# Attention pass of a four-layer graph network: all scatters in bf16 parts, half of the turned one-hots made by ScalarE

## The chip, the cores and the metric

The kernel runs on one core of one Trainium2 chip. The metric is the device time of one execution in microseconds (us), the median of several runs.

## The reference

A graph of 6,250 nodes and 206,250 edges (sorted by destination) passes through four layers, each on the normalized and rectified node features h (64 wide), each added to x. The change concerns the first layer, graph attention with four heads:

```python
h = (x @ W).reshape(n, HEADS, CH)
a_src = jnp.einsum('nhc,hc->nh', h, att_src)
a_dst = jnp.einsum('nhc,hc->nh', h, att_dst)
e = leaky_relu(a_src[src] + a_dst[dst], NEG_SLOPE)
e = jnp.exp(e - m[dst])                      # m: an upper value per node
alpha = e / (segment_sum(e, dst) + 1e-16)
out = segment_sum(h[src] * alpha[:, :, None], dst)
```

The three layers behind it (a mean over neighbours, a weighted sum, and two relational convolutions) are not touched.

## The kernel before, in words

**Windows and groups.** The destinations are cut into 49 windows of 128 nodes (WINDOWS). A first pass sorts the edges so that each window has 50 slots-columns of 128 edges (CPW): one column for each block of 128 source nodes and one more. The columns of a window are handled in six groups (NG) of 10, 8, 8, 8, 8, 8 columns (GS, starting at G0). "Group g of window dx" is written (dx, g) here; it is number dx*6+g. Groups 0 to 2 add into one PSUM bank, groups 3 to 5 into another.

**One group.** Gathering and scattering are matrix products with one-hot matrices.

- SyncE loads the group's codes (two rows, source and destination place, broadcast to 128 partitions) into BC, one of three buffers, number g % 3 (line 533).
- `turned_one_hots` (line 2183) compares them with the partition's own number and so makes the turned one-hots OT, 2 x GS[g] x 128 bf16 values in a partition, in one VectorE instruction (line 2190). It waits for the codes (f_bc), for SyncE's copy of what the same OT buffer held before (f_kept), and for the gather that read it (f_gath).
- SyncE writes the first half of OT to DRAM for the third layer (`keep`, line 523). In SyncE's loop (line 530) the load for (dx, g) waits until the turned one-hots three groups before are made, and right behind it stands the keep of those one-hots.
- TensorE gathers (line 1325 and 1327): per column three products with the parts of h and three with the parts of the destination's table.
- VectorE takes the larger of two scores (`scores`, line 2205), ScalarE the exponential (line 930), VectorE weighs the rows with it (`weigh`, line 2213).
- VectorE makes the untransposed one-hots ODb (`one_hots`, whose instruction stands in the helper `compare`, line 1844).
- TensorE scatters. In groups 0, 1, 3, 4 (g % 3 < 2) the weighed f32 rows are split into three bf16 parts: the first is the upper half of the word, VectorE makes the second (`rest`, line 2222), GpSimd the third (`lowest_part`, line 751), and TensorE runs three bf16 products a column (line 1343). In groups 2 and 5 the rows stay f32 (Wf), ScalarE turns the one-hots into f32 (`one_hots_whole`, line 937) and TensorE runs one f32 product a column (line 1349).
- Three odd edges per partition are added at the window's end (`few` makes their one-hots, line 2235; the products, line 1356), and VectorE adds the two banks to the sums (`evict`, line 2232).

**Order.** Every engine's order is written out by hand; nothing is planned by a program. For each g, TensorE runs the gather of the group three further on and then the scatter of g. VectorE runs (line 2239, `body`): weigh(g); turned one-hots of the group four further on; rest(g) if g % 3 < 2; scores(g+1); one_hots(g+1); and an evict after g = 2 and g = 5, few after g = 3. ScalarE runs, for each g: the slot codes for `one_hots` (line 944) at g = 2 and 5, the exponential of g+1, and `one_hots_whole` of g+1. GpSimd runs the four lowest parts and a small copy of the window's table (line 745). "Step g" below is VectorE's work from weigh(g) up to weigh(g+1).

Of the kernel before, what the change touches and what calls it, by code (L numbers as in the profile page):

```python
# [15 lines left out]
P = 128  # L16
# [4 lines left out]
LASTW = WINDOWS - 1  # L21
# [101 lines left out]
def gnn_stack(nc, x, src, dst, etype, eweight, w0, att_src, att_dst, bias0, gamma0, beta0, w1t, b1, w2t, b2,  # L123
# [11 lines left out]
    with ctx:  # L135
# [179 lines left out]
        OD = cv.take(GS[2] * P).rearrange("p (k n) -> p k n", n=P)  # L315
        WV = DIM + HEADS
        Wf = cv.take(GS[2] * WV).rearrange("p (k c) -> p k c", c=WV)
        W3 = [cv.take(GS[a] * PARTS * WV).rearrange("p (k a c) -> p k a c", a=PARTS, c=WV) for a in range(2)]
# [105 lines left out]
        f_oht, f_ohb, f_ohd, f_gath, f_whole = (sem(n) for n in ("f_oht", "f_ohb", "f_ohd", "f_gath", "f_whole"))  # L424
        f_tab, p_rest, p_low = sem("f_tab"), sem("p_rest"), sem("p_low")
# [44 lines left out]
        def weighed(g):  # L470

            return Wf if g % 3 == 2 else W3[g % 3][:, 0:GS[g], 0, :]

        def in_parts(dx, g):

            return dx * 4 + (g // 3 * 2 + g % 3 + 1)
# [4 lines left out]
        def _(sp):  # L481
# [43 lines left out]
            def load_codes():  # L525
# [18 lines left out]
                for g in range(3, NG):  # L544
                    sp.wait_ge(f_oht, LASTW * NG + g + 4)
                    keep(LASTW, g)
# [48 lines left out]
        def _(pool):  # L595
# [143 lines left out]
            with pool.Else():  # L739
# [19 lines left out]
                lowest_part(0, 1)  # L759
                pool.wait_ge(f_mg, 16 * 2 * MC)  # L760
# [4 lines left out]
                lowest_part(0, 4)  # L765
                pool.wait_ge(f_mexp, 1)
# [5 lines left out]
                with pool.Fori(1, LASTW) as d:  # L772
# [3 lines left out]
                    lowest_part(d, 3)  # L776
                    lowest_part(d, 4)
                for g in (0, 1, 3, 4):
                    lowest_part(LASTW, g)
# [39 lines left out]
        def _(act):  # L819
# [296 lines left out]
        def _(pe):  # L1116
# [190 lines left out]
            def gather(dx, g):  # L1307
# [4 lines left out]
                pe.wait_ge(f_oht, n + 4)  # L1312
# [18 lines left out]
            def scatter(dx, g):  # L1331
# [4 lines left out]
                if g % 3 < 2:  # L1336
                    pe.wait_ge(p_low, in_parts(dx, g))
                    pe.wait_ge(f_ohb, n + 1)
# [1228 lines left out]
```

## Time and profile before

| | us |
|---|---|
| median of 3 runs (4734.94 to 4755.01) | 4735.81 |
| the profiled execution, its own time | 4763.33 |
| its span, first to last instruction | 4761.2 |
| the attention pass in it | about 1030 to 1911 |

The profiled execution is 27.5 us above the median and 2.1 us above its own span. A row of the profile names the line of the kernel, the engine, the operation, what it writes and reads, how often it ran, its busy time, the mean of one in ns, and how long the engine had been idle before it and what released it. PE is TensorE's products, PEld its loads of weights, DVE VectorE, ACT ScalarE, POOL GpSimd, SP SyncE. The recorded duration of an instruction reaches beyond the start of the next one on the same engine by some 0.08 us (VectorE) to 0.09 us (ScalarE), so what an instruction costs its engine is the step from its start to the next start.

### The profile page before, as it was taken

To read this page: it belongs to the slowest core of one execution; us is meant where nothing else is said; L and a number is where in the kernel's file an instruction comes from. 1 tells how busy PE (TensorE), PEld (TensorE's weight loads), DVE (VectorE), ACT (ScalarE), POOL (GpSimd) and SP (SyncE) were. 2 spreads that over 40 slices of the span, in tenths; PEclk is the share of its full clock that TensorE was granted. 3 is DMA by queue.
4 is the path that set the end of the run, shared out by engine and by line. 5 is a ranking of instruction groups with operands and counts; after the bars stand their busy time and mean duration, and the time that the engine had idled before them with its cause. 6 is when DMAs were issued, how large, how long until landed. Compare 5 with 4: busy or idle time off the path is not lost.

```text
span 4761.2 us, 259988 instructions
## 1 busy us (share of the span) xinstructions
PE 4240.2 (89%) x103202; PEld 3795.6 (80%) x103202; DVE 4055.6 (85%) x6401; ACT 3062.0 (64%) x10437; POOL 827.5 (17%) x952
## 2 busy tenths in 40 slices
PE   1899999839999999499969999699999989999998
PEld 1677777639999999488869999588888868888887
DVE  7799999989999999899989999877767766767666
ACT  2899999802222222487779999666666656666665
POOL 2355555413333334000000000000000000000000
PEclk7999999969999999799989999899999989999999
DMA  1000000048888887000025555333333333333333
GB/s 55 2 2 2 2 2 2 2 117 280 276 281 277 280 277 255 15 0 0 0 67 144 147 143 146 89 98 96 98 97 98 97 87 101 99 100 99 101 96 83
DMA packets 305220, 501.36 MB, mean 105 GB/s; under 512 B 76918, under 2 KB 78454, under 8 KB 305126
## 3 DMA queue, kind: packets, MB, share of 16 engines
q1 hardware_dynamic: 303782, 499.39, 35.4%
q8 instruction: 64, 1.05, 0.1%
q0 software_dynamic: 576, 0.52, 0.1%
q10 hardware_dynamic: 768, 0.16, 0.0%
q14 instruction: 30, 0.25, 0.0%
HBM read 408.40 MB, written 91.57 MB: 105 GB/s over the span
## 4 chain that ended last, share of the span: by engine, by line
PE 44%; DVE 24%; issue 13%; ACT 13%; POOL 3%; DVEq 1%; DMA 1%; ACTq 0%; POOLq 0%; SPq 0%
PE PS L1535 20%; ACT arena L869 11%; PE PS L1528 9%; DVE arena L1844 7%; DVE arena L2454 4%; POOL arena L751 3%; PE PS L1327 3%; PE PS L1325 3%; PE PS L1343 2%; DVE arena L2288 2%; DVE arena L2293 2%; PE PS L1349 2%; PE PS L1566 1%; PE PS L1449 1%; PE PS L1464 1%
## 5 line engine op out<-in xcount | busy, mean ns | idle before, releaser
L1844 DVE TENSOR_TENSOR arena<-iotab,arena 128x1024 bf16<-128x1024 bf16 (+4 forms) x1887 | 1605.2, 882 | 188.5 <-PE PS L1535 166.7
L1076 ACT ACTIVATE arena<-PS 128x384 bf16<-128x384 f32 x2450 | 1004.1, 501 | 544.5 <-PE PS L1528 540.9
L1535 PE MATMUL PS<-arena 32*128 32x193 bf16 (+1 forms) x41552 | 998.2, 242 | 47.0 <-DVEq L2455 42.1
L1535 PEld LDWEIGHTS PS<-arena 32*128 32x128 bf16 x41552 | 840.5, 93 | 151.6 <-DVEq L2455 59.1
L869 ACT ACTIVATE arena<-PS,m 128x196 bf16<-128x196 f32 x1813 | 740.6, 445 | 22.0 <-PE PS L1184 21.9
L1528 PE MATMUL PS<-Hp,arena 128*128 128x192 bf16 (+1 forms) x4900 | 537.9, 249 | 35.3 <-DVE Hp L1688 35.0
L1045 ACT ACTIVATE arena<-PS,ewB 128x64 f32<-128x64 f32 x2450 | 526.4, 479 | 34.7 <-PE PS L1388 34.7
L1325 PE MATMUL PS<-Hp,arena 128*128 128x72 bf16 x7350 | 499.2, 198 | 42.1 <-DVE arena L2190 40.9
L1327 PE MATMUL PS<-arena 128*128 128x72 bf16 x7350 | 499.8, 198 | 0.0
L1528 PEld LDWEIGHTS PS<-Hp,arena 128*128 128x128 bf16 x4900 | 383.2, 99 | 146.0 <-issue 84.4
L930 ACT ACTIVATE arena<-arena 128x32 f32<-128x32 f32 (+1 forms) x294 | 68.3, 232 | 648.2 <-DVE arena L2205 645.3
L1191 PE MATMUL PS<-arena,tmp 128*128 128x262 bf16 x1813 | 452.0, 278 | 15.9 <-DVE tmp L1844 13.7
L1184 PE MATMUL PS<-agg,identb 128*128 128x196 bf16 x1813 | 449.9, 248 | 0.0
L1325 PEld LDWEIGHTS PS<-Hp,arena 128*128 128x128 bf16 x7350 | 411.9, 101 | 42.3 <-DVE arena L2190 41.0
L869 ACT ACTIVATION_READ_ACCUMULATOR arena<-PS,m 128x1 f32 x1813 | 412.4, 227 | 0.0
L1327 PEld LDWEIGHTS PS<-arena 128*128 128x128 bf16 x7350 | 405.0, 100 | 0.0
L751 POOL TENSOR_TENSOR arena<-arena 128x680 f32<-128x680 f32 x196 | 325.9, 1663 | 369.8 <-DVE arena L2222 369.0
L1009 ACT ACTIVATE arena<-PS 128x1024 bf16<-128x1024 f32 (+1 forms) x294 | 311.1, 1059 | 94.0 <-PE PS L1449 87.1
L1388 PE MATMUL PS<-Hp,arena 128*128 128x64 bf16 x7350 | 265.0, 194 | 25.0 <-DVE Hp L1688 20.0
L719 POOL DMA_INDIRECT arena<-rows_h,midx x12 | 15.3, 1275 | 1564.3 <-DMA rows_h<-Hn 1516.2
L2454 DVE TENSOR_REDUCE arena<-PS 128x512 f32<-128x1536 f32 x98 | 171.8, 1753 | 129.9 <-PE PS L1535 129.9
L1183 PE MATMUL PS<-Hp,own_b 128*128 128x196 bf16 x1045 | 262.0, 251 | 22.8 <-ACT arena L869 21.2
(374 smaller groups left out, 8298.0 us busy)
## 6 DMA issues: line engine op xcount, KB each, us to landing
arena<-hots SPq DMA_DIRECT2D x735, 256.0 KB, 2.6
arena<-codes SPq DMA_DIRECT2D x245, 512.0 KB, 5.2
hots<-arena SPq DMA_DIRECT2D x245, 256.0 KB, 5.1
arena<-hots SPq DMA_DIRECT2D x147, 320.0 KB
arena<-codes SPq DMA_DIRECT2D x49, 640.0 KB, 5.4
hots<-arena SPq DMA_DIRECT2D x49, 320.0 KB, 5.4
rows_h<-Hn SPq DMA_DIRECT2D x4, 1568.0 KB, 9.2
rows_l<-Y SPq DMA_DIRECT2D x1, 1764.0 KB, 9.8
```

The lines of the kernel that those rows point to most:

```text
L751: pool.tensor_tensor(W3[a][:, 0:n, 2, :], W3[a][:, 0:n, 1, :], W3up[a][:, 0:n, 1, :], ALU.subtract).then_inc(p_low, 1)
L869: act.activation(junk[:, j % 4, :], ps[j % 4][:, 0:KEYS], ACT.Relu, bias=m256[:, 0:1], accum_out=rank[par][:, j:j + 1]).then_inc(k_rank, 1)
L1045: done = act.activation(W3q[g][:, k, 0, :], bank_at(g, k), ACT.Copy, scale=ewB[:, bass.ds(dx * CPW + (G0[g] + k), 1)])
L1076: act.activation(RG[ROW_BUFFER[g]][:, 2 * i:2 * i + 2, 0:RW], ps[PAIR_BANK[q]][:, 0:2 * RW].rearrange("p (k c) -> p k c", k=2), ACT.Copy). ...
L1184: pe.matmul(to, identb[:, j:j + 1].to_broadcast((P, P)), Tb[par], start=False, stop=True).then_inc(k_pref, 1)
L1191: pe.matmul(ps[4][:, 0:EW + 2], OS[:, j, :], E[:, j, 0:EW + 2], start=(j == 0), stop=(j == NJ - 1)).then_inc(k_perm, 1)
L1325: pe.matmul(to, OT[g % 3][:, k * P:(k + 1) * P], rhs, start=(a == 0), stop=False)
L1327: last = pe.matmul(to, OT[g % 3][:, (sz + k) * P:(sz + k + 1) * P], ztab[:, a, :], start=False, stop=(a == PARTS - 1))
L1528: last = pe.matmul(ps[PAIR_BANK[q]][:, (c % 2) * RW:(c % 2 + 1) * RW], rOT[hot][:, (c - G0[hot]) * P:(c - G0[hot] + 1) * P], rhs, start=Tr ...
L1535: last = pe.matmul(ps[2 + q][:, b * SW:b * SW + SW - o], one_hot[32 * q:32 * q + 32, b * P:(b + 1) * P], rows_of[32 * q:32 * q + 32, 0:SW ...
L1844: return dve.tensor_tensor(to.rearrange("p k (n t) -> p k n t", t=4), iota_of[:, 0:n].rearrange("p (n t) -> p n t", t=4)[:, None, :, :] .t ...
L2454: flink(dve.tensor_reduce(Zs.rearrange("p (q b) c -> p q b c", b=2), sums, AX.X, ALU.add))
```

## The change

Groups 2 and 5 are scattered in bf16 parts like the others: the f32 one-hots OD, the rows Wf, `one_hots_whole` and the f32 products go; a third buffer W3[2] comes, and `rest` and `lowest_part` now run for all six groups. The turned one-hots of groups 0, 2 and 4 stay with VectorE. Those of groups 1, 3 and 5 are made by ScalarE: `codes_away` writes the distance |p + 1 - code| over the codes in BC, and `turned_one_hots` writes relu(1 - distance) to OT. Two semaphores (f_away, f_ota) are added; `wait_turned` picks f_oht or f_ota for TensorE and SyncE.

```diff
         def in_parts(dx, g):
-            return dx * 4 + (g // 3 * 2 + g % 3 + 1)
+            return dx * NG + (g + 1)
+
+        def wait_turned(engine, dx, g):
+            engine.wait_ge(f_ota if g % 2 else f_oht, dx * 3 + (g // 2 + 1))
...
# SyncE, load of the codes
                     for g in range(NG):
-                        sp.wait_ge(f_oht, dx * NG + g + 1)
+                        if g >= 3:
+                            wait_turned(sp, dx, g - 3)
+                        elif not first:
+                            wait_turned(sp, dx - 1, g + 3)
...
# GpSimd
-                    lowest_part(d, 3)
-                    lowest_part(d, 4)
+                    for g in range(2, NG):
+                        lowest_part(d, g)
...
# ScalarE
-            def one_hots_whole(dx, g):
-
-                if g % 3 == 2:
-                    act.wait_ge(f_ohb, dx * NG + g + 1)
-                    act.wait_ge(f_scat, dx * NG + g + 1)
-                    act.activation(OD, ODb[2], ACT.Copy).then_inc(f_ohd, 1)
+            def codes_away(dx, g):
+
+                act.wait_ge(f_bc[g % 3], dx * 32 + (g // 3 + 1) * 16)
+                of = BC[g % 3][:, 0:2 * GS[g] * P]
+                act.activation(of, of, ACT.Abs, bias=pidx[:, 1:2], scale=-1.0).then_inc(f_away, 1)
+
+            def turned_one_hots(dx, g):
+
+                act.wait_ge(f_away, dx * 3 + (g // 2 + 1))
+                if g >= 3 or not is_zero(dx):
+                    act.wait_ge(f_kept[g % 3], dx * 32 + g // 3 * 16)
+                act.wait_ge(f_gath, dx * NG + g + 1)
+                m = 2 * GS[g] * P
+                act.activation(OT[g % 3][:, 0:m], BC[g % 3][:, 0:m], ACT.Relu, bias=ones[:, 0:1],
+                               scale=-1.0).then_inc(f_ota, 1)
...
                     slot_codes(cdw, 0, h, None)
+                codes_away(0, 1)
+                turned_one_hots(0, 1)
+                codes_away(0, 3)
+                turned_one_hots(0, 3)
                 exponents(0, 0)
-                one_hots_whole(0, 0)
...
                         if g < NG - 1:
                             exponents(dx, g + 1)
-                            one_hots_whole(dx, g + 1)
                         elif not last:
                             exponents(dx + 1, 0)
-                            one_hots_whole(dx + 1, 0)
+                        if g == 0:
+                            codes_away(dx, 5)
+                        elif g == 1:
+                            turned_one_hots(dx, 5)
+                        elif g % 2 == 0 and not last:
+                            codes_away(dx + 1, g - 1)
+                        elif not last:
+                            turned_one_hots(dx + 1, g - 2)
...
# TensorE, scatter: all groups as g % 3 < 2 before
-                else:
-                    pe.wait_ge(f_whole, n + 3)
-                    pe.wait_ge(f_ohd, dx * 2 + (h + 1))
-                    for k in range(GS[g]):
-                        last = pe.matmul(to, OD[:, k, :], Wf[:, k, :], start=False,
-                                         stop=(g == 2 and k == GS[g] - 1))
...
# VectorE
                         weigh(dx, g)
-                        if g < NG - 4:
-                            turned_one_hots(dx, g + 4)
-                        elif not last:
-                            turned_one_hots(dx + 1, g + 4 - NG)
-                        if g % 3 < 2:
-                            rest(dx, g)
+                        if g == 0:
+                            turned_one_hots(dx, 4)
+                        elif g % 2 == 0 and not last:
+                            turned_one_hots(dx + 1, g - 2)
+                        rest(dx, g)
...
-                for g in range(4):
+                for g in (0, 2):
                     turned_one_hots(0, g)
```

## Rows read from the trace of the kernel before

**Rows 1.** Page, busy us and share of the span by engine

```profile
PE 4240.2 (89%) x103202; PEld 3795.6 (80%) x103202; DVE 4055.6 (85%) x6401; ACT 3062.0 (64%) x10437; POOL 827.5 (17%) x952
```

**Rows 2.** Stretch 1247 to 1423: busy us (instructions) by engine, clock, DMA share, GB/s

```profile
1247.00:1423.00 176.00, 174.04 (x4393) 172.79 (x4390) 176.00 (x311) 38.66 (x100) 70.02 (x50) 1.00 0.87 279
```

**Rows 3.** Line 2235 (`few`, once a window) from 1070 to 1882

```profile
L2235 DVE TENSOR_TENSOR arena<-iota,mrel x46: 1445/1448/1452, 1072.7 to 1866.7; 128x384 f32<-128x384 f32 x46
```

**Rows 4.** Groups by line and form, 1036 to 1911: busy us, mean ns | idle before, releaser

```profile
L751 POOL TENSOR_TENSOR arena<-arena 128x544 f32<-128x544 f32 x147 | 236.1, 1606 | 181.4 <-DVE arena L2222 180.6
L2190 DVE TENSOR_SCALAR arena<-arena,pidx 128x2048 bf16<-128x2048 bf16 x245 | 215.9, 881 | 5.2 <-DMA hots<-arena 3.1 <-DMA arena<-codes 2.1
L1343 PE MATMUL PS<-arena 128*128 128x68 bf16 x4998 | 191.6, 194 | 13.4 <-POOL arena L751 13.3
L751 POOL TENSOR_TENSOR arena<-arena 128x680 f32<-128x680 f32 x49 | 89.8, 1833 | 188.4 <-DVE arena L2222 188.4
L2190 DVE TENSOR_SCALAR arena<-arena,pidx 128x2560 bf16<-128x2560 bf16 x48 | 53.4, 1113 | 0.0
```

**Rows 5.** Chain that ended last, 1490 to 1526: start, us, what

```profile
1492.67 0.76 PE PS L1343 x24
...
1503.76 1.81 PE PS L1349 x16
```

**Rows 6.** VectorE in order of time, parts of steps 2, 3, 5 and 0: start, us

```profile
1491.66 1.11 DVE L2190 TENSOR_SCALAR arena<-arena,pidx 128x2560 bf16<-128x2560 bf16 x1
...
1494.16 0.74 DVE L2190 TENSOR_SCALAR arena<-arena,pidx 128x2048 bf16<-128x2048 bf16 x1
1494.82 0.71 DVE L2222 TENSOR_TENSOR arena<-arena 128x544 f32<-128x544 f32 x1
1495.45 0.21 DVE L2205 TENSOR_REDUCE arena<-PS 128x32 f32<-128x64 f32 x1
1495.59 0.68 DVE L1844 TENSOR_TENSOR arena<-iotab,arena 128x1024 bf16<-128x1024 bf16 x1
1496.19 1.45 DVE L2235 TENSOR_TENSOR arena<-iota,mrel 128x384 f32<-128x384 f32 x1
1497.56 0.68 DVE L2213 TENSOR_TENSOR arena<-PS,arena 128x512 f32<-128x512 f32 x1
...
1501.84 0.81 DVE L1844 TENSOR_TENSOR arena<-iotab,arena 128x1280 bf16<-128x1280 bf16 x1
1502.57 0.21 DVE L2232 TENSOR_TENSOR agg<-agg,PS 128x68 f32 x1
1502.70 0.81 DVE L2213 TENSOR_TENSOR arena<-PS,arena 128x640 f32<-128x640 f32 x1
1503.43 0.74 DVE L2190 TENSOR_SCALAR arena<-arena,pidx 128x2048 bf16<-128x2048 bf16 x1
1504.10 0.85 DVE L2222 TENSOR_TENSOR arena<-arena 128x680 f32<-128x680 f32 x1
1504.87 0.21 DVE L2205 TENSOR_REDUCE arena<-PS 128x32 f32<-128x64 f32 x1
```

**Rows 7.** ScalarE in order of time, the exponential of group 1

```profile
1505.12 0.23 ACT L930 ACTIVATE arena<-arena 128x32 f32<-128x32 f32 x1 [2.93 <-DVE arena L2205]
```

**Rows 8.** SyncE, one load of codes and the keep behind it

```profile
1492.93 0.38 SPq L533 DMA_DIRECT2D arena<-codes  x1
1493.50 0.36 SPq L523 DMA_DIRECT2D hots<-arena  x1
```

**Rows 9.** Line 523 (keep), the whole trace

```profile
DMA to landing us min/median/max: 2.0/5.1/6.7
```

**Rows 10.** Lines of ScalarE, by form: busy us, mean ns

```profile
L937 ACT ACTIVATE arena<-arena 128x1024 f32<-128x1024 bf16 x98 | 103.8, 1059 | 36.0 <-DVE arena L1844 36.0
L930 ACT ACTIVATE arena<-arena 128x32 f32<-128x32 f32 x245 | 56.7, 231 | 614.8 <-DVE arena L2205 611.9 <-PE PS L1343 2.9
L834 ACT ACTIVATE st<-st,epsc 128x28 f32<-128x28 f32 x5 | 1.6, 321 | 1.8 <-DVE st L1652 1.8
L949 ACT ACT_TABLE_LOAD x1 | 1.3, 1283 | 35.2 <-DVEq L2014 35.2
```

**Rows 11.** The pass begins: VectorE in order of time, waiting for first transfers

```profile
1034.83 0.89 DVE L2190 TENSOR_SCALAR arena<-arena,pidx 128x2560 bf16<-128x2560 bf16 x1 [5.49 <-DMA arena<-codes]
1042.45 0.75 DVE L2190 TENSOR_SCALAR arena<-arena,pidx 128x2048 bf16<-128x2048 bf16 x1 [3.11 <-DMA hots<-arena]
```

**Rows 12.** Line 533 (load of codes), its first three, 1020 to 1034

```profile
DMA to landing us min/median/max: 4.7/4.7/4.7
```

More of the change, by code:

```diff
@@ L314, in gnn_stack @@
         ODb = [cv.take(GS[a] * P, bf16).rearrange("p (k n) -> p k n", n=P) for a in range(3)]
-        OD = cv.take(GS[2] * P).rearrange("p (k n) -> p k n", n=P)
         WV = DIM + HEADS
-        Wf = cv.take(GS[2] * WV).rearrange("p (k c) -> p k c", c=WV)
-        W3 = [cv.take(GS[a] * PARTS * WV).rearrange("p (k a c) -> p k a c", a=PARTS, c=WV) for a in range(2)]
+        W3 = [cv.take(GS[a] * PARTS * WV).rearrange("p (k a c) -> p k a c", a=PARTS, c=WV) for a in range(3)]
         W3up = [v.rearrange("p k a c -> p (k a c)").bitcast(bf16).rearrange(
@@ L424, in gnn_stack @@
         f_oht, f_ohb, f_ohd, f_gath, f_whole = (sem(n) for n in ("f_oht", "f_ohb", "f_ohd", "f_gath", "f_whole"))
+        f_away, f_ota = sem("f_away"), sem("f_ota")
         f_tab, p_rest, p_low = sem("f_tab"), sem("p_rest"), sem("p_low")
@@ L544, in load_codes @@
                 for g in range(3, NG):
-                    sp.wait_ge(f_oht, LASTW * NG + g + 4)
+                    wait_turned(sp, LASTW, g)
                     keep(LASTW, g)
@@ L759, in _ @@
                 lowest_part(0, 1)
+                lowest_part(0, 2)
                 pool.wait_ge(f_mg, 16 * 2 * MC)
@@ L765, in _ @@
                 lowest_part(0, 4)
+                lowest_part(0, 5)
                 pool.wait_ge(f_mexp, 1)
@@ L775, in _ @@
                     table_of(d + 1)
-                    lowest_part(d, 3)
-                    lowest_part(d, 4)
-                for g in (0, 1, 3, 4):
+                    for g in range(2, NG):
+                        lowest_part(d, g)
+                for g in range(NG):
                     lowest_part(LASTW, g)
@@ L1311, in gather @@
                 m = sz // 2
-                pe.wait_ge(f_oht, n + 4)
+                wait_turned(pe, dx, g)
                 if g == 0:
@@ L1335, in scatter @@
                 to = ps[4 + h][:, 0:WV]
-                if g % 3 < 2:
-                    pe.wait_ge(p_low, in_parts(dx, g))
-                    pe.wait_ge(f_ohb, n + 1)
-                    if g % 3 == 0:
-                        pe.wait_ge(f_accout, dx * 2 + (h + 1))
-                    for k in range(GS[g]):
-                        for a in range(PARTS):
-                            last = pe.matmul(to, ODb[g % 3][:, k, :], W3up[g % 3][:, k, a, :],
-                                             start=(g % 3 == 0 and k == 0 and a == 0), stop=False)
-                else:
-                    pe.wait_ge(f_whole, n + 3)
-                    pe.wait_ge(f_ohd, dx * 2 + (h + 1))
-                    for k in range(GS[g]):
-                        last = pe.matmul(to, OD[:, k, :], Wf[:, k, :], start=False,
-                                         stop=(g == 2 and k == GS[g] - 1))
+                pe.wait_ge(p_low, in_parts(dx, g))
+                pe.wait_ge(f_ohb, n + 1)
+                if g % 3 == 0:
+                    pe.wait_ge(f_accout, dx * 2 + (h + 1))
+                for k in range(GS[g]):
+                    for a in range(PARTS):
+                        last = pe.matmul(to, ODb[g % 3][:, k, :], W3up[g % 3][:, k, a, :],
+                                         start=(g % 3 == 0 and k == 0 and a == 0),
+                                         stop=(g == 2 and k == GS[g] - 1 and a == PARTS - 1))
                 last.then_inc(f_scat, 1)
@@ L2196, in one_hots @@
                         dve.wait_ge(f_codes, dx * 2 + (g // 3 + 1))
-                    if g % 3 < 2:
-                        dve.wait_ge(f_scat, dx * NG + (g + 1))
-                    elif not (is_zero(dx) and g < 3):
-                        dve.wait_ge(f_ohd, dx * 2 + g // 3)
+                    dve.wait_ge(f_scat, dx * NG + (g + 1))
                     compare(ODb[g % 3][:, 0:GS[g], :], iotab1, cdw[:, G0[g]:G0[g] + GS[g], :]).then_inc(f_ohb, 1)
@@ L2274, in attention_pass @@
                 dve.wait_ge(f_accout, 2 * WINDOWS + 2)
-                dve.sem_inc(f_ohd, 4 * WINDOWS)
+                dve.sem_inc(f_ohd, 6 * WINDOWS)
             def weight_pass():
@@ L2342, in _ @@
             with dve.Else():
-                dve.sem_inc(f_oht, 3)
                 dve.sem_inc(f_whole, 2)
```

3 lines of the change are left out of this document (1 added, 2 removed).

## Prediction, written before the changed kernel was run

> **What bounds the kernel now.** I read the page's first part, then one steady stretch of the attention pass, then the groups of the pass by line, then the order of time on each engine, and the two DMA lines last. Over the whole kernel no engine is full [rows 1]; inside the pass two are: in 176 us VectorE is busy 176.00 and TensorE 174.04, TensorE's granted clock is 1.00 (2.4 GHz), the DMA engines are busy 0.87 of the time and ScalarE only 38.66 us [rows 2]. `few` runs once a window and its starts lie (1866.7 - 1072.7) / 45 = 17.64 us apart [rows 3]: that is the price of a window. VectorE never waits in it, TensorE waits 13.3 us in 49 windows, 0.27 each, for GpSimd [rows 4]. So both engines need some 17.4 to 17.6 us a window, and a change that relieves only one gains nothing. This one relieves both, and loads ScalarE, GpSimd and the turnaround of the buffers.
>
> **TensorE.** An f32 scatter of eight columns occupies it for 1.81 us, a bf16 one in three parts for 0.76 [rows 5]. Two of them change: -2.10. It then needs 17.64 - 0.27 - 2.10 = 15.27 us a window.
>
> **VectorE, without new waits.** Turned one-hots now: five of 2048 elements at 0.881 and one of 2560 at 1.113 [rows 4]; less the overlap of 0.08 that the steps show (0.74 recorded, 0.66 to the next start [rows 6]) that is 5.04 us. The mean is above 0.74 because an instruction that starts while GpSimd's L751 runs is drawn out (the 1.11 of rows 6). After: two of 2048 at 0.66 and one of 2560 at 0.89 - 0.08 = 0.81 [rows 6, 11], 2.13 us; I count no drawing out, since GpSimd's 1.61 us after `rest` are over, or nearly, before the next of them starts. That is -2.91. Two more `rest` at 0.63 [rows 6]: +1.26. In steps 1, 3 and 5 `rest` now stands right behind weigh and waits for its completion: weigh is recorded with 0.68, the next could start after 0.60, and with 0.03 for the signal that is 0.11 each, +0.33. Sum: 17.64 - 2.91 + 1.26 + 0.33 = **16.32 us**.
>
> **ScalarE.** The two f32 one-hots (1059 ns) go. Six instructions of 2048 elements come. Between 32 and 1024 elements an ACTIVATE rises by (1059 - 231) / 992 = 0.835 ns an element, so 2048 take 1059 + 1024 x 0.835 = 1914 ns; the new ones take their bias from a column, and L834, which does, takes 321 ns for 28 elements against 231 for 32: +0.09, so 2.00 us [rows 10]. Bounds: 1.91 without that term, 2.1 with twice the term. Less the overlap of 0.09 that is 6 x 1.91 = 11.5 us, with exponentials and slot codes some 12.7 us a window: not the bound. The Trainium skill, ScalarE: Activation LUTs, "Rules for kernel authors", speaks against such a move: it gives relu-like work to VectorE, up to three times as fast in bf16. The rows agree for one instruction (2.00 against 0.74) and two are needed here; it costs nothing as long as ScalarE's time is spare, but it costs latency, which is the next point.
>
> **The turnaround of the OT buffers.** This is the term that decides. VectorE writes OT for the group four further on, and it must wait until what the buffer held has been written to DRAM (f_kept). Before, the buffer's former content was made three steps earlier by VectorE itself, which left room for the landing of the keep. Now VectorE's one-hots of (dx+2, 0), in step 2 of window dx+1, go into the buffer that ScalarE filled with (dx+1, 3), and ScalarE starts that only behind the exponential of (dx+1, 0), that is after scores at the end of step 5. From the end of those scores:
>
> - exponential: 0.04 until it starts [rows 6, 7], 0.23 - 0.09 until the next can start; the one-hots 2.00 [rows 10];
> - SyncE: the turned one-hots of 1491.66 ended at 1492.77 and the load was issued at 1492.93, so 0.16 [rows 6, 8]; the keep stands 0.57 behind the load [rows 8];
> - landing of the keep 5.1, the median [rows 9]; 0.03 for the signal.
>
> Sum 0.04 + 0.14 + 2.00 + 0.16 + 0.57 + 5.1 + 0.03 = **8.04 us**. VectorE's work from the same moment to those one-hots [rows 6]: one_hots(0) 0.65 left, evict 0.13, weigh(0) 0.73, turned (4) 0.67, rest(0) 0.77, scores 0.14, one_hots(1) 0.60, weigh(1) 0.60, rest(1) 0.11 + 0.63, scores 0.14, one_hots(2) 0.60, weigh(2) 0.60: **6.37 us**. So VectorE waits 8.04 - 6.37 = 1.67 us. The same sum for buffer 1 (filled behind scores(4), wanted in step 0) is 7.61 of work, `few` with 1.37 lying in it, and a wait of 0.43; that wait lies inside the 8.04 of the first and shortens its wait to 1.24, so the total stays 1.67. Buffer 2 has 7.48 and the 1.24: no wait.
>
> A window is then 16.32 + 1.67 = **17.99 us**, against 17.64: +0.35, in the 48 windows that make one-hots for a next one +16.8 us. TensorE (15.27) and the DMA engines (0.87 x 17.64 / 17.99 = 0.85) are below it. GpSimd has 5 x 1.61 + 1.83 [rows 4] and the table's copy, some 10.3 us; groups 2 and 5 now wait for it too, which costs TensorE time that it has.
>
> **The start.** Today VectorE's fourth turned one-hots start at 1042.45, released by a keep [rows 11]. Now they are ScalarE's, and the first exponential stands behind them: their 2.00 against 0.66 puts it back by 1.3 us, and by some 1.9 more if the distance is not finished by then. I take 1.9, between these. The end of the pass I cost at nothing.
>
> **Sum.** +16.8 + 1.9 = +18.7 us. The profiled execution took 4763.3, its successor would take 4782.0; the median of the runs shown stands 27.5 lower, so 4735.8 + 18.7 = **4754.5 us**. The unknown is the landing of the keep: a tenth of a us is worth 4.8 us. Its recorded ends are 2.0 and 6.7 [rows 9]; I take the median, since the load ahead of this keep is the large one but the queue has had some 5 us to empty. The pass's first load, the same 640 KB on an empty queue, needed 4.7 [rows 12]; the keep behind it is issued 0.57 later and adds 256 KB, at 279 GB/s [rows 2] 0.9 us: 4.7 - 0.57 + 0.9 = 5.0.
>
> **Rivals.** About 0.5% (24 us) is what a measurement of this kernel can tell from no change.
>
> 1. *The keep lands in time (faster), 15%.* If it lands in 3.4 us or less the wait is gone, and VectorE's 16.32 set the window: 48 x -1.32 + 1.9 = -61, 4674 us. For it: in the fast case nothing is queued. Against it: medians of 5.1 now, and 4.7 for a transfer on an empty queue. Over 4.2 us the gain is within 0.5%. The Trainium skill, DMA: Bandwidth & Descriptors, "Anatomy of one DMA", gives about 2.0 us plus bytes at 436 GB/s; by it load and keep together would need 4.1 us, the keep 3.5 from its own issue, and the window would be 16.4 us, 4679 us in all, an estimate from that page. The trace disagrees where it can be compared: that page makes 3.5 us of the first load, the row 4.7.
> 2. *The keeps land later (slower), 36%.* ScalarE ends odd one-hots after VectorE has ended the next even ones, so SyncE sends two loads and two keeps in a row, 1664 KB within 1.6 us. If they share the DMA engines instead of following each other, the keep lands a us later, 6.1, still under the 6.7 seen; the window is 18.99 and the time 4735.8 + 64.8 + 1.9 = 4802 us. It decides from 5.2 us on, where +0.5% is reached, very near my forecast; hence its large share.
> 3. *Table loads, 2%.* If Abs or Relu needed another table than Exp, each change of table would cost 1.28 us [rows 10], two a group: ScalarE would need 12.7 + 12 x 1.28 = 28.1 us a window, +500 us, 5238 us. Against it: Copy and Exp alternate in this pass, and the one load is ahead of it [rows 10]. The Trainium skill, ScalarE: Activation LUTs, "Table sets: the hidden batching unit", has relu and abs in every set.
>
> **How the numbers follow.** My forecast, a keep landing between 4.2 and 5.2 us, has 47%, and its own range is 4712 to 4760. Rival 1 has 15%, rival 2 36%, rival 3 2%. Faster by over 0.5%: 0.15; within: 0.47; slower: 0.38. The range reaches into rival 1 to 4702 (a landing of 4.0) and to 4802 for rival 2; the bounds of ScalarE's instruction (-0.09 to +0.1, 5 us) lie inside.
>
> **What would show it.** VectorE's L2190 with idle time ahead of it, released by the DMA that writes `hots`, about 1.2 us in step 2 and 0.4 in step 0; `few` 18.0 us apart; ScalarE's new lines at 2.0 us; SyncE's transfers in pairs; TensorE idle over 2 us a window; no ACT_TABLE_LOAD in the pass. VectorE without idle time and 16.3 us between the `few`s would make the forecast wrong, as would waits for scores or exponentials.

## The result, and the profile after

The changed kernel takes **4836.47 us** (median of 4 runs, 4831.0 to 4838.03) against 4735.72 for the kernel before beside it: a ratio of 1.0202 [1.0183, 1.0221]. It is slower by 2.0%, and outside the range of the prediction (4702 to 4802). The profiled execution took 4838.03 us, with a span of 4836.3.

The page's first part and the stretch of the pass answer to [rows 1, 2]; the window is read from `few`, now line 2252, as in [rows 3]. Columns as there.

```profile
PE 4159.9 (86%) x103986; PEld 3705.7 (77%) x103986; DVE 4035.7 (83%) x6352; ACT 3520.0 (73%) x10633; POOL 962.6 (20%) x1050
...
1250.00:1426.00 176.00, 147.18 (x4204) 143.54 (x4205) 158.33 (x276) 123.55 (x130) 89.73 (x65) 0.99 0.83 258
...
L2252 DVE TENSOR_TENSOR arena<-iota,mrel x46: 1442/1443/1446, 1075.3 to 1944.3; 128x384 f32<-128x384 f32 x46
```

No engine is full any more: in 176 us TensorE went from 174.04 to 147.18 and VectorE from 176.00 to 158.33. The window is (1944.3 - 1075.3) / 45 = **19.31 us** where 17.99 was forecast. At the granted clock of 0.99 the TensorE clock has no part in this. The first `few` starts at 1055.3, where it was 1055.0, and the last at 1981.3, where it was 1900.6: 80.7 us later, 80.4 of them in the 48 windows. After it the kernel is shorter by 5.6. So the whole loss arose in the pass. The windows are not alike: from one `few` to the next it is 18.6 to 20.2 us, but for the last, so what one stretch of the trace shows lies about the mean.

The groups of the pass by line and form, 1036 to 2000 (as [rows 4]; 2239 is `rest`, 2210 VectorE's turned one-hots, 944 and 953 ScalarE's two steps, 1368 the scatter in three parts):

```profile
L2239 DVE TENSOR_TENSOR arena<-arena 128x544 f32<-128x544 f32 x245 | 218.4, 891 | 5.1
...
L953 ACT ACTIVATE arena<-arena,ones 128x2048 bf16<-128x2048 bf16 x147 | 294.3, 2002 | 0.4
L944 ACT ACTIVATE arena<-arena,pidx 128x2048 bf16<-128x2048 bf16 x147 | 292.1, 1987 | 6.7 <-DMA arena<-codes 6.7
...
L2210 DVE TENSOR_SCALAR arena<-arena,pidx 128x2560 bf16<-128x2560 bf16 x48 | 42.5, 886 | 67.1 <-DMA hots<-arena 63.2 <-PE PS L1353 3.1 <-DMA arena<-codes 0.8
L2210 DVE TENSOR_SCALAR arena<-arena,pidx 128x2048 bf16<-128x2048 bf16 x98 | 72.9, 744 | 28.3 <-DMA hots<-arena 25.3 <-DMA arena<-codes 2.1 <-issue 0.4
```

Two things stand here. VectorE waits 63.2 + 25.3 = 88.5 us for transfers that write `hots`, some 1.8 us a window. And the mean `rest` of 544 elements takes 891 ns, where the one of [rows 6] took 0.71: 245 x 0.18 = 44 us, 0.9 a window, that no wait shows.

VectorE in order of time, parts of steps 4, 5 and 0 to 2 (as [rows 6]):

```profile
1497.76 0.71 DVE L2239 TENSOR_TENSOR arena<-arena 128x544 f32<-128x544 f32 x1
...
1499.84 0.90 DVE L2239 TENSOR_TENSOR arena<-arena 128x544 f32<-128x544 f32 x1
1500.66 0.23 DVE L2222 TENSOR_REDUCE arena<-PS 128x40 f32<-128x80 f32 x1
...
1503.24 0.75 DVE L2210 TENSOR_SCALAR arena<-arena,pidx 128x2048 bf16<-128x2048 bf16 x1 [0.74 <-DMA hots<-arena]
...
1505.42 0.68 DVE L2230 TENSOR_TENSOR arena<-PS,arena 128x512 f32<-128x512 f32 x1
1506.13 1.12 DVE L2239 TENSOR_TENSOR arena<-arena 128x544 f32<-128x544 f32 x1
...
1510.39 0.89 DVE L2210 TENSOR_SCALAR arena<-arena,pidx 128x2560 bf16<-128x2560 bf16 x1 [1.80 <-DMA hots<-arena]
```

GpSimd beside it, in order of time:

```profile
1492.81 1.09 POOL L757 TENSOR_TENSOR arena<-arena 128x544 f32<-128x544 f32 x1
...
1498.55 1.61 POOL L757 TENSOR_TENSOR arena<-arena 128x544 f32<-128x544 f32 x1 [2.39 <-DVE arena L2239]
...
1504.85 1.83 POOL L757 TENSOR_TENSOR arena<-arena 128x680 f32<-128x680 f32 x1 [2.27 <-DVE arena L2239]
```

The `rest` at 1497.76 has no GpSimd work beside it and takes 0.71. Those at 1499.84 and 1506.13 start while line 757 of the group before still runs, and end late: 1506.13 begins inside 1504.85 to 1506.68 and ends at 1507.25, which is 0.57 after GpSimd's end, nearly a whole `rest` (0.63 by its cadence). That is the pattern of the 1.11 of [rows 6]. GpSimd is held up in its turn: the same 544 elements take it 1.09 or 1.61. Every `rest` now has line 757 of the group before close by, and in the odd steps, where no turned one-hots of VectorE stand between, the two meet.

ScalarE and SyncE from the end of the scores at 1500.89, the path that the prediction rests on (as [rows 7, 8]), and the landing of the keep, line 526, over the trace (as [rows 9]):

```profile
1500.93 0.24 ACT L938 ACTIVATE arena<-arena 128x40 f32<-128x40 f32 x1
1501.14 2.00 ACT L953 ACTIVATE arena<-arena,ones 128x2048 bf16<-128x2048 bf16 x1
...
1503.31 0.38 SPq L539 DMA_DIRECT2D arena<-codes  x1
1503.89 0.36 SPq L526 DMA_DIRECT2D hots<-arena  x1
1504.49 0.38 SPq L539 DMA_DIRECT2D arena<-codes  x1
1505.06 0.42 SPq L526 DMA_DIRECT2D hots<-arena  x1
1509.87 0.38 SPq L539 DMA_DIRECT2D arena<-codes  x1
...
DMA to landing us min/median/max: 2.3/5.9/7.3
```

The chain is the forecast one, to the step: exponential, ScalarE's second step, load, keep, landing, and VectorE's one-hots at 1510.39 behind 1.80 us of idle time. The transfers go in pairs, with nothing for 4.8 us after them. The median keep lands 5.9 us after its issue, where it was 5.1 before; the keep of this window, issued at 1503.89, took 6.50 to the one-hots.

### The profile page after: what moved, and what is told of

The parts are those of the page before. It is cut to its first block, busy times and chain, and to the rows that moved or that the text cites. A ratio compares the mean times of both kernels' runs of the same rounds, so it can differ in the third digit from the quotient of the medians.

```text
span 4836.3 us, 261743 instructions
## 1 busy us (share of the span) xinstructions
PE 4159.9 (86%) x103986; PEld 3705.7 (77%) x103986; DVE 4035.7 (83%) x6352; ACT 3520.0 (73%) x10633; POOL 962.6 (20%) x1050
## 3 DMA queue, kind: packets, MB, share of 16 engines
q8 instruction: 64, 1.05, 0.1%
## 4 chain that ended last, share of the span: by engine, by line
PE 38%; DVE 23%; issue 17%; ACT 13%; POOL 5%; DMA 2%; DVEq 1%; ACTq 0%; POOLq 0%; SPq 0%
PE PS L1555 20%; ACT arena L877 12%; PE PS L1548 9%; DVE arena L1864 6%; POOL arena L757 5%; DVE arena L2469 4%; DVE arena L2304 2%; DVE arena L2309 2%; PE PS L1368 2%; PE PS L1353 1%; PE PS L1351 1%; DMA hots<-arena 1%; PE PS L1586 1%; PE PS L1484 1%; PE PS L1469 1%
## 5 line engine op out<-in xcount | busy, mean ns | idle before, releaser
L757 POOL TENSOR_TENSOR arena<-arena 128x544 f32<-128x544 f32 (+1 forms) x294 | 466.1, 1585 | 320.7 <-DVE arena L2239 320.7
L1368 PE MATMUL PS<-arena 128*128 128x68 bf16 x7350 | 285.6, 195 | 166.6 <-POOL arena L757 165.6
L1353 PEld LDWEIGHTS PS<-arena 128*128 128x128 bf16 x7350 | 408.7, 101 | 0.0
L1368 PEld LDWEIGHTS PS<-arena 128*128 128x128 bf16 x7350 | 252.0, 97 | 186.5 <-POOL arena L757 141.5
L944 ACT ACTIVATE arena<-arena,pidx 128x2048 bf16<-128x2048 bf16 x147 | 292.1, 1987 | 6.7 <-DMA arena<-codes 6.7
L953 ACT ACTIVATE arena<-arena,ones 128x2048 bf16<-128x2048 bf16 x147 | 294.3, 2002 | 0.4
```

The lines of the kernel that those rows point to most:

```text
L757: pool.tensor_tensor(W3[a][:, 0:n, 2, :], W3[a][:, 0:n, 1, :], W3up[a][:, 0:n, 1, :], ALU.subtract).then_inc(p_low, 1)
L1353: last = pe.matmul(to, OT[g % 3][:, (sz + k) * P:(sz + k + 1) * P], ztab[:, a, :], start=False, stop=(a == PARTS - 1))
L1368: last = pe.matmul(to, ODb[g % 3][:, k, :], W3up[g % 3][:, k, a, :], start=(g % 3 == 0 and k == 0 and a == 0), stop=(g == 2 and k == GS[g] ...
```

## The experiments

The theory: a window is VectorE's work (16.3 us, with `few` in it at 1.37), plus two terms: the turnaround of the OT and BC buffers, and the drawing out of VectorE's instructions beside GpSimd's third parts. The rivals: that the turnaround alone makes the loss; that TensorE's waits for GpSimd (165.6 us in the pass) do; that the place of `rest` does. The diffs are against the changed kernel (that of run 12 against run 8), cut to their core. Runs 1 to 4, 5 to 8 and 9 to 12 went together, with medians of the kernel before of 4747.2, 4736.9 and 4737.7; across these sets compare the ratios, since the first had the kernel before 10 us slower.

| run | median us | ratio to before | window us |
|---|---|---|---|
| changed kernel | 4836.5 | 1.0202 [1.0183, 1.0221] | 19.31 |
| 1 six OT buffers | 4815.4 | 1.0142 [1.0116, 1.0167] | 18.79 |
| 2 six OT, six BC | 4760.0 | 1.0026 [1.0013, 1.0038] | 17.61 |
| 3 `rest` late | 4821.3 | 1.0155 [1.0130, 1.0181] | 18.90 |
| 4 runs 2 and 3 together | 4775.7 | 1.0053 [1.0030, 1.0077] | 17.97 |
| 5 bf16 parts alone | 4854.8 | 1.0245 [1.0219, 1.0270] | 19.70 |
| 6 ScalarE's one-hots alone | 4842.7 | 1.0220 [1.0195, 1.0246] | 19.38 |
| 7 run 2, short third parts | 4699.0 | 0.9915 [0.9890, 0.9940] | 16.59 |
| 8 run 2, group 2 in f32 | 4716.2 | 0.9953 [0.9938, 0.9969] | 16.79 |
| 9 before, unchanged | 4742.0 (one) | - | 17.28 |
| 10 table copy later | 4836.1 | 1.0207 [1.0190, 1.0224] | 19.33 |
| 11 run 2, table copy later | 4734.9 | 0.9991 [0.9978, 1.0004] | 17.21 |
| 12 run 8, whole one-hots later | 4688.5 | 0.9896 [0.9880, 0.9913] | 16.26 |

**1. Six OT buffers, so that no one-hots wait for a keep of the same window.**

```diff
         OT = [cv.take(2 * GS[0] * P, bf16) for _ in range(3)]
+        in_tmp = tmp[:, :, :].rearrange("p w c -> p (w c)")
+        OT += [in_tmp[:, n * GS[3] * P:(n + 1) * GS[3] * P].bitcast(bf16) for n in range(3)]
...
-                if g >= 3 or not is_zero(dx):
-                    act.wait_ge(f_kept[g % 3], dx * 32 + g // 3 * 16)
-                act.wait_ge(f_gath, dx * NG + g + 1)
+                if not is_zero(dx):
+                    act.wait_ge(f_kept[g], dx * 16)
+                    act.wait_ge(f_gath, dx * NG + g - 2)
```

> The changed kernel with six OT buffers in place of three (three of them in a tensor that is idle in this pass), so that one-hots wait for a keep that is a window old. Theory (the window is set by the way from ScalarE's exponential over its one-hots and the keep to VectorE's next one-hots, 8.85 us in the trace, of which VectorE waits 2.05): the keep leaves the way and the load of codes, issued 0.57 us earlier and landing some 0.3 sooner, takes its place: 8.0 us, the wait falls to about 1.2, the window from 19.29 to 18.4, the time to about 4794 us. Rival 1 (only the keep matters): no wait left, 17.2 us, 4738. Rival 2 (the drawn-out rests and GpSimd set the pace): no change, 4836.

The waits for `hots` are gone, but the window fell by 0.52 us only. By form, VectorE's turned one-hots of group 0 now wait for the codes, 42.9 us in place of 63.2:

```profile
L2212 DVE TENSOR_SCALAR arena<-arena,pidx 128x2560 bf16<-128x2560 bf16 x48 | 43.2, 901 | 47.4 <-DMA arena<-codes 42.9 <-PE PS L1355 4.5
```

The BC buffer has the same turnaround, one transfer earlier in the queue; a wait had stood behind the wait. The time missed its expectation by some 20 us, and more drawing out goes with it: the compare of one_hots has a mean of 718 ns, against 677 where it is undisturbed (run 10).

**2. Six OT and six BC buffers; SyncE loads a window ahead.**

```diff
+        in_Y = Y[:, :, :].rearrange("p w c -> p (w c)")
+        BC += [in_Y[:, n * GS[3] * P:(n + 1) * GS[3] * P].bitcast(bf16) for n in range(3)]
...
+                        wait_turned(sp, dx, g)
+                        if not last:
+                            load(dx + 1, g)
+                        keep(dx, g)
```

> Six OT and six BC buffers; SyncE loads the codes of a group for the next window as soon as its one-hots are made. Theory: no wait is left on VectorE, the window is VectorE's own work with the rests drawn out, 16.32 + 0.91 = 17.2 us, the time 4836 - 48 x 2.05 = about 4738 us, DMA share about 0.93. Rival (the DMA engines, busy 0.83 of 19.3 us = 16.0 us a window, are the bound once transfers can queue): window 17.2 or more with VectorE waiting for codes.

But for one wait at the start of the pass VectorE no longer waits for a transfer, and the window fell by 1.70 us, to 17.61. That is the price of the turnaround: the 2.0 us of waits of the changed kernel, less what the drawing out takes back. It is 0.4 above the 17.2 expected, since more is drawn out than in the changed kernel: the mean `rest` of 544 elements takes 1002 ns, where it was 891. In order of time, VectorE and GpSimd:

```profile
1499.83 0.97 DVE L2213 TENSOR_SCALAR arena<-arena,pidx 128x2048 bf16<-128x2048 bf16 x1
1500.72 1.61 DVE L2242 TENSOR_TENSOR arena<-arena 128x544 f32<-128x544 f32 x1
...
1498.85 2.90 POOL L760 TENSOR_TENSOR arena<-arena 128x544 f32<-128x544 f32 x2
```

GpSimd had waited for the table's copy; its two third parts then run in one, 1498.85 to 1501.75, and VectorE's one-hots take 0.97 in place of 0.74 and the `rest` 1.61 in place of 0.71, ending 0.58 after GpSimd.

**3. `rest` behind scores and one_hots of the next group, in the odd steps.**

```diff
-                        rest(dx, g)
+                        if g % 2 == 0:
+                            rest(dx, g)
                         if g < NG - 1:
                             scores(dx, g + 1)
                             one_hots(dx, g + 1)
...
+                        if g % 2:
+                            rest(dx, g)
```

> The changed kernel with three buffers of each, but in the odd steps VectorE runs rest behind scores and one_hots of the next group, when GpSimd has ended the third part of the group before. Theory: the rests fall from 0.90, 1.13 and 1.02 to 0.71 us (-0.91) and the 0.11 behind weigh go (-0.33), but what of it lies on the way to the keep (0.41 + 0.11) turns into waiting: -0.7 us a window, 4836 - 35 = about 4801 us. Rival 1 (a shared port between VectorE and GpSimd does not explain the long rests, or they only moved): no change. Rival 2 (the third parts come later and hold TensorE up): slower than 4836.

By form (1864 is the compare of one_hots):

```profile
L1864 DVE TENSOR_TENSOR arena<-iotab,arena 128x1024 bf16<-128x1024 bf16 x245 | 196.6, 803 | 0.0
L2239 DVE TENSOR_TENSOR arena<-arena 128x544 f32<-128x544 f32 x245 | 177.6, 725 | 0.1
```

The `rest`s are back at 725 ns, and the compares rose instead, to 803 where an undisturbed one takes 677 (run 10). `few` came down to 0.55 in most windows, and the waits for `hots` rose to take that up. The drawing out moved to whatever stands next to GpSimd's work; the window gained 0.41 us where the theory gave it 0.7.

**4. Runs 2 and 3 together.**

> Both together: six OT and BC buffers, and rest behind one_hots in the odd steps. Theory: VectorE's work alone, 16.0 us a window, would give 4836 - 48 x 3.3 = 4678 us; the DMA engines need 16.0 us as well, so 16.0 to 16.9 and 4678 to 4722 us, faster than the kernel before. Rival (GpSimd's chain or TensorE, 15.3 us, binds): over 17 us, with TensorE's scatters waiting for L757 and VectorE waiting for the scatters.

A clear miss: the window was 17.97, slower than run 2 without the move. In its trace the drawing out stands at the turned one-hots (means of 1333 and 973 ns in place of 0.89 and 0.74) and at the `rest`s (894 ns). The theory that the place of `rest` is to blame falls with runs 3 and 4: which instruction is hit depends on the order, that some are hit does not.

**5. bf16 parts alone: all turned one-hots by VectorE, as before the change.**

```diff
         def wait_turned(engine, dx, g):
-            engine.wait_ge(f_ota if g % 2 else f_oht, dx * 3 + (g // 2 + 1))
+            engine.wait_ge(f_oht, dx * NG + (g + 1))
...
+                        if g < NG - 4:
+                            turned_one_hots(dx, g + 4)
+                        elif not last:
+                            turned_one_hots(dx + 1, g + 4 - NG)
```

> First half of the change alone: all six groups scattered in bf16 parts, all turned one-hots still made by VectorE. Theory: VectorE is the bound. Of its 17.64 us before, 1.8 are drawing-out by GpSimd (0.94 on turned one-hots, 0.89 on few); two more rests are +1.27 and two more third parts draw out more, 0.4 to 0.9: 19.3 to 19.8 us a window, +80 to +105 us against the kernel before, no waits for DMA. Rival (relieving TensorE by 2.1 us a window is worth something by itself): not slower than before.

```profile
1250.00:1426.00 176.00, 150.23 (x4095) 146.90 (x4096) 176.00 (x296) 17.59 (x72) 94.39 (x63) 0.94 0.81 250
...
1309.94 1.44 DVE L1852 TENSOR_TENSOR arena<-iotab,arena 128x1024 bf16<-128x1024 bf16 x1
```

VectorE is busy all of the 176 us and waits for no transfer: the window is 19.70. This part by itself puts 2.06 us on the 17.64 of [rows 3] (2.42 on the 17.28 of run 9). The two `rest`s are 1.27 of it; turned one-hots stand between weigh and `rest` in every step here, so there are no completion waits. Most of what is left is one compare of one_hots, in step 3, that takes 1.44 us in place of 0.68, in 42 windows. Half the change, then, only costs where VectorE is the bound; TensorE's 2.10 us went into idle time.

**6. ScalarE's one-hots alone: groups 2 and 5 scattered in f32, with their one-hots converted by ScalarE.**

```diff
+            def one_hots_whole(dx, g):
+
+                if g not in IN_PARTS:
+                    act.wait_ge(f_ohb, dx * NG + g + 1)
+                    act.wait_ge(f_scat, dx * NG + g + 1)
+                    act.activation(OD, ODb[2], ACT.Copy).then_inc(f_ohd, 1)
...
                             exponents(dx, g + 1)
+                            one_hots_whole(dx, g + 1)
```

> Second half alone: turned one-hots of groups 1, 3 and 5 by ScalarE in two steps, groups 2 and 5 scattered in f32 as before. Theory: VectorE's own work is 14.1 us, 1.3 more with GpSimd's drawing-out, and the way to the keep is the same 8.9 us, so some 2.1 us of waiting: 17.5 us a window; TensorE needs 17.4. So 17.4 to 17.9, within 0.5% of the kernel before. Rival 1 (without the way to the keep): the same, set by TensorE alone, and VectorE never waits for hots. Rival 2 (ScalarE, now 14.6 us busy, sets it): VectorE waits for L930's successor, over 18 us.

The window was 19.38 where 17.4 to 17.9 had been expected. ScalarE in order of time, and VectorE's weigh behind it:

```profile
1313.20 1.06 ACT L946 ACTIVATE arena<-arena 128x1024 f32<-128x1024 bf16 x1 [0.37 <-DVE arena L1881]
1314.16 1.99 ACT L952 ACTIVATE arena<-arena,pidx 128x2048 bf16<-128x2048 bf16 x1
1316.06 0.27 ACT L969 ACTIVATE arena<-cdA 128x96 bf16 x1
1316.23 0.22 ACT L939 ACTIVATE arena<-arena 128x40 f32<-128x40 f32 x1
...
1316.48 0.82 DVE L2247 TENSOR_TENSOR arena<-PS,arena 128x640 f32<-128x640 f32 x1 [1.55 <-ACT arena L939]
```

The scores of group 0 end at 1313.91, and their exponential starts at 1316.23, 2.3 us later, since ScalarE works in order and is in the middle of long instructions. VectorE waits 1.55 us for it, and all that follows on the path of the keep is late by as much. In the changed kernel the exponential starts 0.04 behind the scores. Of the difference, 1.34 us is ScalarE's: with the f32 one-hots in between (1.06, and 0.37 of waiting for them), it is 3.63 us from one exponential to the next (1312.60 to 1316.23), against 2.29 (1498.64 to 1500.93) in the changed kernel. The other 0.94 is VectorE's, which has no `rest` in step 5 and so ends its scores earlier. So the two halves need each other, and each alone is no better than both (1.0245, 1.0220, 1.0202).

**7. Run 2, with the third part made by GpSimd for the first column only; those of the other columns are left out.**

```diff
+                    n = 1
                     pool.tensor_tensor(W3[a][:, 0:n, 2, :], W3[a][:, 0:n, 1, :], W3up[a][:, 0:n, 1, :],
```

> Six OT and BC buffers as in e2_both6, and GpSimd computes the third part of the first column of each group only (the third parts of the other columns are left out, so TensorE adds stale values there). Theory (GpSimd's tensor_tensor draws out VectorE's instructions that read two operands from SBUF or run at the fast rate, about 2 us a window wherever they stand): rests 0.71, few 0.55, turned one-hots 0.74 all together, the window 15.4 to 16.2 us, bound by TensorE (15.3), the DMA engines (about 15.4 to 16) and VectorE (15.4) alike: 4760 - 48 x 1.4 to 2.2 = 4655 to 4693 us. Rival (the long rests come from ScalarE's accesses or from their own order): rests stay at 0.9 to 1.6, time near 4760.

```profile
L761 POOL TENSOR_TENSOR arena<-arena 128x68 f32<-128x68 f32 x294 | 181.6, 630 | 348.8 <-DVE arena L2243 348.8
...
L2243 DVE TENSOR_TENSOR arena<-arena 128x544 f32<-128x544 f32 x245 | 181.3, 740 | 5.2
```

With GpSimd's instructions down from about 1.6 to 0.63 us, the `rest`s take 740 ns, where they took 1002 in run 2, `few` 0.55 and the turned one-hots 0.75 to 0.88, and the window goes from 17.61 to 16.59. That misses the 15.4 to 16.2 expected. Most of the drawing out is gone: VectorE's instructions are shorter by some 1.8 us a window than in run 2. Waits for TensorE's scatters took part of its place (38.3 us in the pass against 9.2, 0.6 a window). So the drawing out is worth at least 1.0 us a window here. This shows GpSimd's work to be its cause: VectorE's and ScalarE's instructions are the same in both runs.

**8. Run 2, with group 2 alone in f32.** The edit is that of run 6, with IN_PARTS = (0, 1, 3, 4, 5), on run 2.

> Six OT and BC buffers, group 5 in bf16 parts, group 2 in f32 as in the kernel before (GpSimd has five third parts, VectorE five rests). Theory: VectorE 14.8 us and some 1.7 of drawing-out, TensorE 15.27 + 1.05 = 16.3 and its waits: 16.5 to 17.0 us a window, 48 x 0.6 to 1.1 below e2_both6: 4707 to 4731 us, faster than the kernel before. Rival (what holds e2 at 17.6 is the DMA engines): near 4760, VectorE or ScalarE waiting for codes.

It came out at 16.79 us a window, 0.9953 of before. What VectorE waits for now is the exponential (line 943, 44.8 us in 50 waits), which stands behind ScalarE's f32 one-hots.

**9. The kernel before, unchanged, for a second profile.**

> The kernel before, unchanged, for a second profile: its timed runs lie at 4734 to 4763 us and the first profile was taken in one of 4763. Theory (the drawing-out by GpSimd depends on where its third parts fall among VectorE's instructions, and the loop can settle in more than one pattern): if this run is again near 4760, the same 17.64 us a window; if it is near 4735, some 17.1 us a window, with few or a turned one-hot shorter. Rival (the difference lies in another stage): 17.64 us a window in a run near 4735, and another stage some 25 us shorter.

`few` is 17.28 us apart over the same 45 windows that give 17.64 in [rows 3], and takes 0.55 us, not 1.45:

```profile
L2235 DVE TENSOR_TENSOR arena<-iota,mrel x48: 541/550/1450, 1073.3 to 1884.8; 128x384 f32<-128x384 f32 x48
...
1505.34 0.55 DVE L2235 TENSOR_TENSOR arena<-iota,mrel 128x384 f32<-128x384 f32 x1
1505.81 0.68 DVE L2213 TENSOR_TENSOR arena<-PS,arena 128x512 f32<-128x512 f32 x1
1506.41 1.23 DVE L2190 TENSOR_SCALAR arena<-arena,pidx 128x2048 bf16<-128x2048 bf16 x1
```

One kernel settles into more than one pattern. In this one GpSimd meets the turned one-hots (1.23), in the one of [rows 6] it meets `few` (1.45). From the first `few` to the last it is 829.9 us against 845.6, so 15.7 less, and the whole executions differ by 21 (4763.3 and 4742.0). The timed runs of the kernel before fall apart in the same way: of the nine beside runs 5 to 8, seven lie at 4733.5 to 4737.6 and two at 4755.3 and 4756.9. At 17.28 TensorE is full (176.00 us of the 176 from 1250 to 1426), where it was busy 174.04 in [rows 2].

**10. The table's copy behind the third part of group 2, three buffers.**

```diff
                     lowest_part(d, 1)
+                    lowest_part(d, 2)
                     table_of(d + 1)
-                    for g in range(2, NG):
+                    for g in range(3, NG):
                         lowest_part(d, g)
```

> The changed kernel with three buffers of each and one step of GpSimd moved: the table's copy, which waits for a gather, stands behind the third part of group 2 in place of ahead of it, so that TensorE's scatter of group 2 need not wait for both. TensorE's waits for GpSimd (165 us in the pass) should shrink by some 40 to 80 us. Theory (the way to the keep sets the window): these waits cover nothing, the time stays at 4836 within 10 us. Rival (GpSimd's chain holds TensorE up and that sets the window): over 20 us faster.

The time is unchanged, as the theory said. But it is a weak test of the rival: TensorE's waits for line 757, which should have shrunk by 40 to 80 us, stayed as they were (165.7 us in 141 waits, against 165.6 in 142), and only GpSimd's own wait for the gather went. That TensorE's waits are slack rests on the changed kernel's own trace, where VectorE waits for the gather and the scatters some 8 us in the whole pass and 88.5 for the keeps, and on run 2, where the window fell by 1.70 us with the same third parts.

**11. Run 2 with the edit of run 10.**

> Six OT and BC buffers as in e2_both6, with the same move of the table's copy. Without the way to the keep, VectorE waited 0.14 us a window there for TensorE's scatters, and the pattern jumped between windows (17.61 on average, up to 0.35 about it). Theory: 17.2 to 17.6 us a window, 4740 to 4760 us. Rival (GpSimd's chain was the hidden bound of e2): under 17.0, under 4731 us.

```profile
L2243 DVE TENSOR_TENSOR arena<-arena 128x544 f32<-128x544 f32 x245 | 207.2, 846 | 5.1
```

Without the transfers' waits the same edit is worth 0.40 us a window, at the upper end of what was expected (17.2 to 17.6 us): GpSimd's two third parts no longer run in one, and the 1.61 of run 2 is gone. At 0.9991 [0.9978, 1.0004] it is level with the kernel before. `few` is drawn out again, to 1.44.

**12. Run 8, with ScalarE's f32 one-hots of group 2 behind the exponential of group 3.**

```diff
                             exponents(dx, g + 1)
-                            one_hots_whole(dx, g + 1)
+                            if g == 2:
+                                one_hots_whole(dx, 2)
```

> As e8_hybrid2 (six buffers, group 2 in f32, group 5 in parts), but ScalarE turns the one-hots of group 2 into f32 behind the exponential of group 3 in place of ahead of the distances' second step. In e8 VectorE waited 0.9 us a window in weigh(3) for that exponential (L943). Theory: that wait goes, TensorE with 16.3 us of work and its own waits is the bound: 16.4 to 16.6 us a window, 4716 - 48 x 0.2 to 0.4 = 4697 to 4706 us. Rival (the f32 one-hots come too late for TensorE): not faster than 4716.

```profile
1250.00:1426.00 176.00, 176.00 (x4850) 176.00 (x4847) 174.90 (x314) 152.47 (x162) 88.60 (x66) 1.00 0.95 303
```

16.26 us a window and 4688.5 us, 0.9896 [0.9880, 0.9913] of before, somewhat better than expected (16.4 to 16.6), and the time beats both kernels. TensorE is full, VectorE 174.90 of 176 and the DMA engines 0.95: this keeps most of the change, with one group left in f32, one long instruction of ScalarE out of the exponentials' way, and buffers for all six groups.

## Why the prediction was wrong

Of the mechanism one half was right: a new wait for `hots`, in steps 0 and 2, on the path named, is the largest single cost. The other half, the drawing out of the `rest`s, was left out. Of the 82 us by which the number was off, 39 are the path, its landing above all, 24 the drawing out and 26 the base; 7 go the other way. Against the steps:

- **TensorE -2.10, not the bound.** Right: 147.18 of 176 us, its idle time put down to line 757 above all. Its recorded busy time fell by only 1.3 us a window (17.44 to 16.15), but that also counts the end of a scatter that nothing overlaps (0.93 recorded, 0.76 to the next start). Run 12, where TensorE is full and one f32 group adds 1.05, bears the sum out: 15.27 + 1.05 = 16.32, and it runs at 16.26.
- **VectorE's 16.32 us.** What was summed held: the completion waits are 0.11 each, as forecast (1506.13 - 1505.42 = 0.71 against 0.60). But it was not all undisturbed work, since `few` stands in it with 1.37 where it costs 0.47 by itself (1505.34 to 1505.81 in run 9). **"I count no drawing out, since GpSimd's 1.61 us after `rest` are over, or nearly"** is the step of the mechanism that failed. It was true of the turned one-hots, which it spoke of (744 and 886 ns), and it was never asked of the `rest`s, which the change sets next to one another. The three `rest`s of the odd steps take 0.82, 1.05 and 0.94 by their cadence in place of 0.635: +0.91 us a window.
- **The path of 8.04 us.** Measured over 44 windows it is 8.85: 0.03 and 0.22 to the start of ScalarE's second step (0.04 and 0.14 forecast), 2.00 for it, 0.74 to the keep's issue (0.73 forecast), and 5.85 from there to the one-hots, where 5.1 and 0.03 had been taken. **"Landing of the keep 5.1, the median"** is the term that was most mis-sized, by 0.7 us or some 35 us in all; I took the value from a queue in which transfers came one at a time. Why it rose stays open. The wait is 8.85 less VectorE's 6.37 + 0.41 (part of the drawing out lies on the way): 2.07, and it was 2.04, in steps 0 and 2 (0.57 and 1.47, where 0.43 and 1.24 had been forecast).
- **The window.** 16.32 + 0.91 + 2.04 = 19.27, against 19.31 measured. The miss, 0.81 of the path and 0.50 of drawing out that does not lie on it, is 1.31 us and makes 48 x 1.31 = 63 us. The start cost 0.3 us and not 1.9, and behind the last `few` 5.6 us fell away that I had left as they were: 4782.0 + 63 - 1.6 - 5.6 = 4837.8 for the profiled execution, which took 4838.0.
- **The base.** I worked out a difference to the profiled execution and set it on the median, 27.5 us lower. But that execution was in the pattern of 17.64 us, and the time of 4742 of run 9 goes with 17.28. Against that pattern, the forecast window of 17.99 would have been +0.71 and not +0.35. The base accounts for 26 of the 82 us (27.5, less the 1.6 by which the profiled execution of the changed kernel is above its median), the other 56 being those above. That the median goes with 17.28 is inferred from run 9 and the two groups of timed runs; no execution at 4735.8 was profiled.
- **Rival 2** described the transfers in pairs (seen), a keep landing one us later (0.75 seen) and 18.99 us a window. It came nearest, and lacked the drawing out. That the pairs cause the later landing stays open: in run 6 SyncE works in pairs too, and there the keep took 5.13 to the one-hots (mean of 44 windows), and no run issued the keep ahead of its load.
- **Rival 1** fell: no keep of the path landed in 3.4 us (4.86 to 6.79 in the 44 windows). The 3.5 us from the keep's issue that went with it is below every one of them. The Trainium skill, DMA: Bandwidth & Descriptors, "Anatomy of one DMA", gives the formula behind that estimate for transfers that GpSimd issues, and these are SyncE's, so neither this nor the first load tests it.
- **Rival 3** fell: ScalarE's new lines take 1987 and 2002 ns (2.00 forecast), with no table load in the pass.

What I should have read is a rule of the Trainium skill, SBUF — State Buffer, "Who interferes with whom": a VectorE instruction with two inputs in SBUF contends with a GpSimd instruction that reads SBUF, one in a two-port performance mode contends with GpSimd too, and whichever comes first keeps the other out until it ends. The trace agrees: the `rest` of 1506.13 ends 0.57 us after GpSimd's, the one of run 2 0.58 after, and weigh, which has one of its two inputs in PSUM, is never drawn out (679 to 681 ns in runs 1, 3 and 10 alike). In the rows of before it stood in the open, at the one-hots of 1491.66 and at `few` [rows 6], whose 1.45 us I took for its length.

## What to carry to other kernels

Where VectorE is the bound, count its instructions that may meet GpSimd's (two inputs in SBUF, or a fast mode), and take GpSimd's time as VectorE's in part; moving VectorE's instruction mostly chose another victim (runs 3 and 4), moving one of GpSimd's was worth 0.40 us a window (run 11), and shortening them 1.0 (run 7). When a producer is moved to a slower or busier engine, write out the whole way until its buffer is free again, with the landing time of the pattern that will be, and look for the buffer that waits behind the first (run 1). And take a difference and the time that it is added to from the same pattern of the loop: one profile may show a pattern that the median does not have.

## What was not expected of the hardware

- A 384-element f32 compare on VectorE takes 0.55 us by itself and 1.45 beside GpSimd, a 544-element f32 subtraction 0.71 and in most windows of run 2 once 1.61, a 2048-element one-hot in bf16 0.74 and 1.21 in the kernel before, 1.30 in run 12. GpSimd's own instruction on 544 elements takes 1.09 to 1.76: 1.76 at 1500.82 in the changed kernel, where a compare of VectorE's starts with it.
- The same program ran its loop at 17.28 and at 17.64 us a window in two executions. What differs in the two traces is which instructions meet GpSimd's, and TensorE is full only at 17.28; what chooses between them stays open.
- A keep of 256 KB needed 5.1 us (median; 5.3 in run 9) when transfers went one by one with the DMA engines at 0.87, and 5.8 when they went two and two at 0.83: a lower mean load and a later landing.
